# Layer 0 attention: the last query tile of all four heads of a quad turned by VectorE and sent through DRAM, and the token-shift difference of the second norm made in place

## Chip, cores, metric

One core of one Trainium2 chip. The metric is the device time of one execution in microseconds (us), the median of several runs.

## What is computed

Two adaptive-layernorm layers follow each other on x of 8 batches, 512 tokens, 256 features. Only the first one is touched. Cut to what matters:

```python
h = layernorm(x) * (1 + ca) + sa
q, k, v = heads(h @ q_w), heads(h @ k_w), heads(h @ v_w)      # 16 heads of 16
scores = q @ k.T / 4 - slope[h] * |i - j|                     # causal, 512 x 512 for each head
x = x + ga * (softmax(scores) @ v) @ o_w
h = layernorm(x) * (1 + cb) + sb
h_prev = shift h by one token, zeros first
xr = mu_r * h + (1 - mu_r) * h_prev                           # = h_prev + mu_r * (h - h_prev)
xk = mu_k * h + (1 - mu_k) * h_prev
x = x + gb * sigmoid(xr @ W_r.T) * (square(relu(xk @ W_k.T)) @ W_v.T)
```

The second layer (local and linear attention, an MLP, four times over; then grouped attention and a mixture of experts) makes up the rest of the time and keeps its code.

## The kernel before

Everything is float32. Each engine has its own instruction stream, written out by hand, and waits on semaphores. Layer 0 runs over slots: slot n = 4b + q works on batch b and on quad q, four heads at a time, 32 slots in all, and a few short slots behind them finish the last batches. A slot holds three kinds of work that are interleaved.

Of its own quad, per slot n. TensorE makes the scores in three units (`scores`, L746), whose PSUM banks S are shared: unit 0 is query tile 3 (four heads, 512 keys wide), unit 1 is tiles 2 and 0 (384 and 128 wide), unit 2 is tile 1 (256 wide). Each unit overwrites banks that the unit before it filled, so it waits for VectorE to have read them. VectorE reads them in `shifted` (L510): one custom instruction per head and tile adds the mask, writes the sum to `prob` and gives the row minimum. ScalarE exponentiates in place (`exps`, L649). At the end of the slot VectorE turns the first three heads of tile 3 in 32x32 blocks into `wide_blocks` (`turn_wide`, L520).

Of the quad before, m = n - 1. The softmax weights must lie key by query for the product with v. Head 3 of tile 3 and all heads of tiles 2, 0 and 1 are turned by TensorE (`turn_probs`, L762, one 128x128 transpose per key block) in eight groups, the list `TURNED`, into two PSUM banks H that alternate; each group is copied to SBUF by ScalarE (groups in `ON_ACT`) or VectorE (`evacuate`, L294), and the group after next waits for that copy. The three heads turned by VectorE go to DRAM and back on SP's queue (`move_wide`, L353 four writes, L358 one read), which puts the 32x32 blocks where they belong (`wideT`). TensorE then forms the product with v for all of them (`values`, L782, "AV"), the last large work of the slot.

Of other batches, six `parts` of one or two steps a slot (`work_of`): projections Q, K, V of the next batch, the turning and normalising of the attention's output (OT, BT, OUT), the second norm's transposes (L2), and the feed-forward products (KF, RF, VF). They use two banks M in turn, and a step waits for the step two before it to be read out. The steps read out by VectorE are OT (L534, L535), OUT (L544, L547) and VF (L565, L568).

So within a slot TensorE's stream is: scores unit 0, groups 0 and 1, part 0, groups 2 and 3, part 1, group 4, part 2, scores unit 1, groups 5 and 6, part 3, group 7, scores unit 2, part 4, part 5 with AV. VectorE's is: `shifted` of two heads of tile 3, group 1, the other two heads, part 0, norm, part 1, group 3, part 2, `shifted` of tiles 2 and 0, part 3, group 6, `shifted` of tile 1, part 4, `turn_wide`, statistics (L485, L488), norm (L496), `mixed` (L556), part 5.

Of the feed-forward part, GpSimd makes `diff` = h - h_prev (L434) in slots with q = 1, VectorE makes xk from it at the end of that slot and xr at the end of the next (`mixed`), and KF and RF read them from `mixT`.

Of the kernel before, what the change touches and what calls it, by code (L numbers as in the profile page):

```python
# [22 lines left out]
P = 128  # L23
B = 8
T = 512
NT = T // P
D = 256
KD = D // P
# [95 lines left out]
SLOTS = B * QUADS  # L124
ORDER_T = (3, 2, 0, 1)
FROM = (0, P, 3 * P, 6 * P)
ROUND = 3
SQUARE = 32
GROUPS = P // SQUARE
WIDE = ROUND * NT  # L130
TURNED = [(3, j, 1) for j in range(ROUND, 4)] + [(2, j, 1) for j in range(4)] + [(0, 0, 4)] + [(1, j, 2) for j in (0, 2)]
ON_ACT = (0, 2, 4, 5, 7)
PTS = len(TURNED)


# [57 lines left out]
def layer0(c, d, start):  # L193
    nc = c.nc
    s = c.s
    with ExitStack() as st:
        def sb(name, shape, dt=F32):
            return st.enter_context(nc.sbuf_tensor(name, shape, dt))
# [3 lines left out]
        mu = sb("mu0", [P, 2, KD])  # L202
        h2T = sb("h2T0", [P, KD, T + 1])
        mixT = sb("mixT0", [P, 2, KD, T])
        diff = sb("diff0", [P, KD, T])
        kact = sb("kact0", [P, KD, T])
        rsig = sb("rsig0", [P, NT, D])
        wqkv = sb("wqkv0", [P, 3, KD, D])
# [18 lines left out]
        tmp = spare[:, 7168:8192].rearrange("p (i t n) -> p i t n", i=2, n=D)  # L227
        wideT = probT[:, 0:P * WIDE].rearrange("p (i k r) -> p i k r", i=GROUPS, r=SQUARE)
        lowT = probT[:, P * WIDE:P * WIDE + 4 * 768].rearrange("p (j n) -> p j n", j=4)
        lastT = probT[:, P * WIDE + 4 * 768:4 * 1280].rearrange("p (j n) -> p j n", n=T)  # L230
        by_block = "p (k n) -> p k n"
        wm = [[spare[:, 7168:8192].rearrange(by_block, k=KD), spare[:, 5120:6144].rearrange(by_block, k=KD),
               spare[:, 6144:7168].rearrange(by_block, k=KD)], [mixT[:, 0], mixT[:, 1], kact[:, :, :]]]
        wide = "p i n -> p (i n)"
        rows = [[gates[0:B, 0].rearrange(wide), gates[0:B, 1].rearrange(wide), rsig[0:B, 2:4, :].rearrange(wide)],
                [diff[0:B, 0, :], diff[0:B, 1, :], rsig[0:B, 0:2, :].rearrange(wide)]]
        sign = tmp[0:B, 0, 0, :]
        qP = [c.prob[:, 4 * i:4 * i + 4, :] for i in range(2)]
        kP = [c.probT[:, 4 * i:4 * i + 4, :] for i in range(2)]
# [45 lines left out]
        def evacuate(eng, copy, m, k):  # L285

            tile, j, nj = TURNED[k]
            at = PTS * m + k
            eng.wait_ge(s["pt_full0"], at + 1)
            if m:  # L290
                full(eng, ("AV", m - 1, 0))
            width = P * (tile + 1)
            dst = lowT[:, j:j + nj, FROM[tile]:FROM[tile] + width] if tile < 3 else lastT[:, j - ROUND:j - ROUND + nj, :]
            copy(dst,  # L294
                 H[at % 2][:, 0:nj * width].rearrange("p (j n) -> p j n", j=nj))\
                .then_inc(s[("pt_out0", "pt_out1")[at % 2]], 1)

        @block.sync
        def _(sp):
# [47 lines left out]
            def move_wide(m):  # L347
                sp.wait_ge(s["wide_turned"], ROUND * (m + 1))
                if m:
                    sp.wait_ge(s["wide_in"], 16 * m)  # L350
                for i in range(GROUPS):
                    src = blocks[SQUARE * i:SQUARE * (i + 1), :, :, :].rearrange("p a k r -> p a (k r)")
                    sp.dma_start(c.probs_dram[0][:, :, i, :].rearrange("a p n -> p a n"), src)\  # L353
                      .then_inc(s["wide_away"], 16)
                sp.wait_ge(s["wide_away"], 16 * GROUPS * (m + 1))
                if m:
                    full(sp, ("AV", m - 1, 0))
                sp.dma_start(wideT.rearrange("p i k r -> p (i k r)"),  # L358
                             c.probs_dram[0].rearrange("a p i n -> (a p) (i n)")).then_inc(s["wide_in"], 16)

            for n in range(SLOTS + 2 * QUADS):
                b, q = divmod(n, QUADS)
# [26 lines left out]
        def _(pool):  # L389
# [35 lines left out]
            for n in range(ALL_SLOTS):  # L425
                b, q = divmod(n, QUADS)
                side = side_of(n)
                for f in side["norm"]:
                    rstd(f, "statsf", "rstdf")
                for f in side["diff"]:  # L430
                    drained(pool, ("L2", 0, f))
                    drained(pool, ("L2", 1, f))
                    pool.wait_ge(s["mixed_ready"], 2 * f)
                    nc.gpsimd.tensor_tensor(diff[:, :, :], h2T[:, :, 1:T + 1], h2T[:, :, 0:T], ALU.subtract)\  # L434
                      .then_inc(s["diff_ready"], 1)
                for f in side["square"]:
                    drained(pool, ("KF", 0, f))
                    drained(pool, ("KF", 1, f))
                    nc.gpsimd.tensor_tensor(kact[:, :, :], kact[:, :, :], kact[:, :, :], ALU.mult)\
                      .then_inc(s["squared_ready"], 1)  # L440
                for f in side["gate"]:
                    drained(pool, ("RF", 0, f))
                    drained(pool, ("RF", 1, f))
                    pool.wait_ge(s[("gb_loaded0", "gb_loaded1")[f % 2]], 16 * (f // 2 + 1))
                    steps(nc.gpsimd.tensor_scalar(rsig[:, :, :], rsig[:, :, :], 1.0, 0.5, ALU.add, ALU.mult))
                    row = gates[:, 1, f % 2:f % 2 + 1, :].to_broadcast([P, NT, D])
                    nc.gpsimd.tensor_tensor(rsig[:, :, :], rsig[:, :, :], row, ALU.mult).then_inc(s["gated0"], 1)
                if q == 0 and b + 2 < B:
                    rstd(b + 2)

        @block.vector
        def _(dve):
# [47 lines left out]
            def shifted(n, u, i, heads):  # L500

                tile, at = UNITS[u][i]
                width = P * (tile + 1)
                dve.wait_ge(s["scores_full"], 3 * n + u + 1)
                for j in heads:
                    if n and tile == 3 and j < ROUND:
                        dve.wait_ge(s["wide_turned"], ROUND * (n - 1) + j + 1)
                    elif n:
                        dve.wait_ge(s["pt_full0"], PTS * (n - 1) + 1 + turn_of(tile, j))
                    nc.vector.tensor_tensor_reduce(out=prob[:, j, FROM[tile]:FROM[tile] + width],  # L510
                                                   in0=S[:, j, at:at + width], in1=mask[:, T - width:T], scale=1.0,
                                                   scalar=3e38, op0=ALU.add, op1=ALU.min,
                                                   accum_out=least[:, n % 2, tile, j:j + 1]).then_inc(s["least0"], 1)
# [84 lines left out]
            for n in range(ALL_SLOTS):  # L598
# [18 lines left out]
                    shifted(n, 1, 0, range(4))  # L617
                    shifted(n, 1, 1, range(4))
                taken(parts[3])
                turned(m, (6,))  # L620
                if live:
                    shifted(n, 2, 0, range(4))
                taken(parts[4])
# [17 lines left out]
        def _(act):  # L641
# [61 lines left out]
            for n in range(ALL_SLOTS):  # L703
# [10 lines left out]
                    exps(n, 0, 0, (2, 3))  # L714
                turned(m, (4,))
                taken(parts[2])
                turned(m, (5,))
                if live:
                    exps(n, 1, 0, range(4))
                taken(parts[3])  # L720
                turned(m, (7,))
                if live:
                    exps(n, 1, 1, range(4))
                taken(parts[4])
# [5 lines left out]
        def _(pe):  # L730
# [35 lines left out]
            def values(m, bank):  # L766
# [3 lines left out]
                for tile in range(NT):  # L770
                    if tile == 3:
                        pe.wait_ge(s["wide_in"], 16 * (m + 1))
                    for key in range(tile + 1):
                        for j in range(4):
                            src = FROM[tile] + P * key
                            if tile < 3:
                                moving = lowT[:, j, src:src + P]
                            elif j < ROUND:
                                moving = wideT[:, :, NT * j + key, :]
                            else:  # L780
                                moving = lastT[:, j - ROUND, P * key:P * key + P]
                            ins = nc.tensor.matmul(bank[32 * j:32 * j + 32, tile * P:(tile + 1) * P],  # L782
                                                   vt[:, b % 2, key, 4 * q + j, :], moving,
                                                   start=(key == 0), stop=(key == tile), tile_position=(0, 32 * j))
# [92 lines left out]
            for n in range(ALL_SLOTS):  # L877
# [15 lines left out]
                if live:  # L893
                    scores(n, 1)
                if turns:
                    turn_probs(m, (5, 6))
                work(parts[3])
                if turns:
                    turn_probs(m, (7,))
                if live:  # L900
                    scores(n, 2)
                work(parts[4])
# [1893 lines left out]
```

## Time and profile before

| | |
|---|---|
| median of 3 runs | 2836.78 us (2836.17 to 2840.8) |
| the profiled execution | 2835.08 us, its span 2833.1 us |
| mean granted TensorE clock | 0.982 of full |
| busy, share of span | PE 96%, DVE 61%, ACT 49%, POOL 29% |
| the 32 slots | first scores at 29.9 us, slot 31 ends at 543.3 us |
| a full batch of four slots | 65.38 us (298.39 to 363.77 us) |

PE is TensorE's matmuls, PEld its weight loads, DVE VectorE, ACT ScalarE, POOL GpSimd. A row of the timeline gives start, duration, engine, line, operation, how many instructions are merged in it, and in brackets how long the engine was idle before it and what released it. A float32 matmul shows as two records, a transpose as one. Matmuls overlap their neighbours, so a merged row is about 0.1 us longer than the step from its start to the next start. A row of the windows has the stretch, its length, the busy time of PE, PEld, DVE, ACT and POOL with instruction counts, the granted clock (1.00 is 2.4 GHz, 0.50 is 1.2 GHz), the DMA share and GB/s.

### The profile page before, as it was taken

The numbers are of one execution on the slowest core, as the hardware profiler recorded it, in microseconds if no ns is written. First come the engines' busy times: TensorE is split into PE (matmuls) and PEld (weight loads), VectorE is DVE, ScalarE is ACT, GpSimd is POOL, SyncE is SP. The second block draws the span as 40 slices with busy tenths as digits, with TensorE's granted clock in tenths as the row PEclk, the third lists the DMA queues.
The fourth block names the chain that finished last, engine by engine and source line by source line (L and its number), as shares of the span: only waits on it lengthen the run. The fifth ranks groups of instructions, "written<-read, shape, count | busy, mean of one in ns | idle before, by whom it ended". The sixth has DMA issues, their size and how long they took to land. (4 is left out here: it accounts for less than half of the span.)

```text
span 2833.1 us, 50970 instructions
## 1 busy us (share of the span) xinstructions
PE 2706.5 (96%) x19124; PEld 1808.2 (64%) x19124; DVE 1727.5 (61%) x5112; ACT 1378.7 (49%) x3081; POOL 820.5 (29%) x830
## 2 busy tenths in 40 slices
PE   7999999887999999999999999999999887899998
PEld 4667776654566666666666666666666444578886
DVE  5888887778766555556565656566745788711113
ACT  4777777524554545555555454545541332322224
POOL 1001111124433332323232333333331210045551
PEclk9999999998999999999999999999999988999999
DMA  6544443325545455545455555454540000123325
GB/s 191 134 122 109 120 124 105 100 75 173 162 120 158 134 167 158 159 126 168 139 168 152 149 155 149 145 156 129 145 124 26 12 16 30 60 68 82 74 76 200
DMA packets 241380, 344.48 MB, mean 122 GB/s; under 512 B 25635, under 2 KB 174118, under 8 KB 237024
## 3 DMA queue, kind: packets, MB, share of 16 engines
q1 hardware_dynamic: 232304, 320.71, 39.0%
q0 software_dynamic: 7680, 16.32, 2.3%
q10 hardware_dynamic: 1152, 4.19, 0.4%
q8 instruction: 152, 2.49, 0.4%
q14 instruction: 92, 0.75, 0.1%
HBM read 184.61 MB, written 152.67 MB: 119 GB/s over the span
## 5 line engine op out<-in xcount | busy, mean ns | idle before, releaser
L1664 PE MATMUL bank<-w,gT 128*128 128x256 f32 x2048 | 463.5, 382 | 2.6 <-ACT gT L1582 2.6
L1631 PE MATMUL bank<-h2T,w 128*128 128x512 f32 x1024 | 444.7, 592 | 0.0
L1664 PEld LDWEIGHTS bank<-w,gT 128*128 128x128 f32 x2048 | 383.8, 190 | 75.9 <-issue 24.9
L1582 ACT ACTIVATE gT<-bank,vec 128x512 f32<-128x512 f32 x256 | 175.9, 687 | 389.6 <-PE bank L1631 389.6
L1631 PEld LDWEIGHTS bank<-h2T,w 128*128 128x128 f32 x1024 | 194.6, 190 | 231.3 <-issue 229.6
L1216 POOL TENSOR_TENSOR prob<-prob,rsum 128x512 f32<-128x512 f32 (+1 forms) x256 | 233.2, 933 | 212.7 <-DVE rsum L1428 211.6
L510 DVE CUSTOM_DVE_ANT_0 y<-bank,mask 128x128 f32<-128x128 f32 (+3 forms) x512 | 219.6, 484 | 64.5 <-PE bank L746 64.1
L649 ACT ACTIVATE y<-y,least 128x128 f32<-128x128 f32 (+3 forms) x512 | 248.4, 560 | 10.7 <-DVE least L510 10.6
L1405 DVE CUSTOM_DVE_ANT_0 prob<-bank,mask 128x256 f32<-128x256 f32 (+1 forms) x512 | 164.3, 387 | 124.3 <-PE bank L1619 124.3
L1523 ACT ACTIVATE prob<-prob,least 128x256 f32<-128x256 f32 (+1 forms) x512 | 238.7, 469 | 1.8 <-DVE least L1405 1.8
L1602 PE MATMUL bank<-wtok,hT 128*128 128x512 f32 x512 | 225.3, 592 | 2.1 <-ACT hT L1514 1.3
L2542 DVE COPY yout<-bank 128x512 f32<-128x512 f32 x40 | 27.7, 692 | 257.0 <-PE bank L2674 250.3
L1602 PEld LDWEIGHTS bank<-wtok,hT 128*128 128x128 f32 x512 | 97.1, 190 | 124.2 <-issue 122.5
L1246 POOL TENSOR_TENSOR tok<-tok,qinv 128x512 f32<-128x512 f32 x32 | 43.7, 1365 | 415.3 <-DVE qinv L1386 415.3
L1302 DVE STREAM_TRANSPOSE prob_blocks<-prob 128x1024 f32<-128x1024 f32 (+1 forms) x128 | 141.3, 1104 | 15.1 <-POOL prob L1216 15.0
L1281 DVE TENSOR_SCALAR xn<-y,mv,rstd 128x256 f32<-128x256 f32 x256 | 88.5, 408 | 98.7 <-POOL rstd L1197 98.7
L762 PEld LDWEIGHTS bank<-ident,y 128*128 128x128 f32 x896 | 102.7, 143 | 71.4 <-issue 57.2
L1287 DVE STREAM_TRANSPOSE score<-xn 128x1024 f32<-128x1024 f32 x63 | 78.5, 1245 | 113.2 <-DMA turned_rows<-score 109.0
L2662 PE MATMUL bank<-inT,we 128*128 128x256 f32 x640 | 144.8, 379 | 2.5 <-ACT inT L2593 1.3
L2601 ACT ACTIVATE score<-bank 128x512 f32<-128x512 f32 x80 | 47.8, 597 | 204.3 <-PE bank L2662 204.3
L762 PE MATMUL bank<-ident,y 128*128 128x128 f32 x896 | 132.9, 281 | 12.8 <-DVE probT L294 6.6
L2674 PE MATMUL bank<-we,score 128*128 128x256 f32 x640 | 144.6, 379 | 0.0
(337 smaller groups left out, 4862.9 us busy)
## 6 DMA issues: line engine op xcount, KB each, us to landing
probT<-turned_probs SPq DMA_DIRECT2D x64, 768.0 KB, 5.0
turned_probs<-prob_blocks SPq DMA_DIRECT2D x128, 256.0 KB, 5.5
probT<-turned_probs SPq DMA_DIRECT2D x32, 1024.0 KB, 5.9
turned_rows<-score SPq DMA_DIRECT2D x252, 128.0 KB, 2.9
score<-turned_rows SPq DMA_DIRECT2D x63, 512.0 KB, 3.9
turned_probs<-wide_blocks SPq DMA_DIRECT2D x128, 192.0 KB, 3.1
turned_probs<-prob_blocks SPq DMA_DIRECT2D x128, 192.0 KB, 3.1
w<-in_W SPq DMA_DIRECT2D x8, 1024.0 KB, 8.4
```

Of the source, the lines that this page charges most:

```text
L510: nc.vector.tensor_tensor_reduce(out=prob[:, j, FROM[tile]:FROM[tile] + width], in0=S[:, j, at:at + width], in1=mask[:, T - width:T], scal ...
L649: ins = nc.scalar.activation(one, one, ACT.Exp, bias=least[:, n % 2, tile, j:j + 1], scale=-1.0)
L762: ins = nc.tensor.transpose(H[at % 2][:, col:col + P], prob[:, j0 + j, src:src + P], c.ident[:, :])
L1216: nc.gpsimd.tensor_tensor(two, two, rsum[:, at:at + 2].unsqueeze(2).to_broadcast([P, 2, width]), ALU.mult).then_inc(s["probs"], 1)
L1405: nc.vector.tensor_tensor_reduce(out=prob[:, at, from_col(q):PAIR], in0=S[:, j, off:off + width], in1=mask[:, from_col(q):PAIR], scale=1.0 ...
L1523: nc.scalar.activation(one, one, ACT.Exp, bias=least[:, at:at + 1], scale=-1.0, accum_out=sums[:, at:at + 1]).then_inc(s["exped"], 1)
L1582: nc.scalar.activation(gT[:, m, :], M[m % 2][:, :], ACT.Gelu, bias=vec[:, h // B, 4 * KD + m:4 * KD + m + 1])\
L1602: ins = nc.tensor.matmul(S[:, t, :], hT[:, k, 1 + t * P:1 + (t + 1) * P], wtok[:, k, :], start=(k == 0), stop=(k == KD - 1))
L1631: ins = nc.tensor.matmul(M[m % 2][:, :], w1[:, k, m * P:(m + 1) * P], h2T[:, k, :], start=(k == 0), stop=(k == KD - 1))
L1664: ins = nc.tensor.matmul(M[i][:, (t % 2) * D:(t % 2 + 1) * D], gT[:, m, t * P:(t + 1) * P], w2[:, m, :], start=(m == 0), stop=(m == MF - 1))
L2662: ins = nc.tensor.matmul(UP[(2 * j + i) % 4][:, (m % 2) * CHUNK_T:(m % 2 + 1) * CHUNK_T], w1[e % 2][:, k, m * P:(m + 1) * P], inT[j % 2][: ...
L2674: ins = nc.tensor.matmul(DOWN[j % 2][:, t * D:(t + 1) * D], gT[j % 2][:, k, t * P:(t + 1) * P], w2[e % 2][:, k, :], start=(k == 0), stop=( ...
```

## The change

- `ROUND` goes from 3 to 4: VectorE turns head 3 of tile 3 too (`turn_wide`, 128 x 512), and its product with v reads `wideT` like the others. The first entry of `TURNED` goes: TensorE no longer makes those four 128x128 transposes, ScalarE no longer copies their 128 x 512 result.
- The seven groups left move up: the slot's stream on TensorE has groups 0 and 1 (now three transposes each), 2 and 3, 4 (now the four of tile 0), and between scores unit 1 and unit 2 only group 5 and group 6. ScalarE copies groups 0, 2, 4 and 6, VectorE 1, 3 and 5 (of the same sizes as before).
- The transfers through DRAM grow by a third: four writes of 256 KB instead of 192 KB, one read of 1024 KB instead of 768 KB, through the other, larger scratch tensor.
- `diff` gets no tile of its own but lies in `mixT[:, 0]`, which the previous batch's RF reads; GpSimd waits for that RF, and xr is made in place over the difference. The rows of the modulation that lay in `diff` lie in `spare_rows` and `tmp`.

```diff
-ROUND = 3
+ROUND = 4
-TURNED = [(3, j, 1) for j in range(ROUND, 4)] + [(2, j, 1) for j in range(4)] + [(0, 0, 4)] + [(1, j, 2) for j in (0, 2)]
-ON_ACT = (0, 2, 4, 5, 7)
+TURNED = [(2, j, 1) for j in range(4)] + [(0, 0, 4)] + [(1, j, 2) for j in (0, 2)]
+ON_ACT = (0, 2, 4, 6)
...
-        diff = sb("diff0", [P, KD, T])
+        spare_rows = sb("spare_rows", [P, T])
...
-                [diff[0:B, 0, :], diff[0:B, 1, :], rsig[0:B, 0:2, :].rearrange(wide)]]
+                [spare_rows[0:B, :], tmp[0:B, 1].rearrange(wide), rsig[0:B, 0:2, :].rearrange(wide)]]
+        diff = mixT[:, 0]
...
-            dst = lowT[...] if tile < 3 else lastT[:, j - ROUND:j - ROUND + nj, :]
+            dst = lowT[:, j:j + nj, FROM[tile]:FROM[tile] + width]
...
-                    sp.dma_start(c.probs_dram[0][:, :, i, :].rearrange("a p n -> p a n"), src)\
+                    sp.dma_start(c.probs_dram[1][:, :, i, :].rearrange("a p n -> p a n"), src)\
...
+                    if f:
+                        full(pool, ("RF", 1, f - 1))
                     nc.gpsimd.tensor_tensor(diff[:, :, :], h2T[:, :, 1:T + 1], h2T[:, :, 0:T], ALU.subtract)\
...
-                    if n and tile == 3 and j < ROUND:
+                    if n and tile == 3:
                         dve.wait_ge(s["wide_turned"], ROUND * (n - 1) + j + 1)
...
(VectorE)      turned(m, (6,)) -> turned(m, (5,))
(ScalarE)      turned(m, (5,)) is gone, turned(m, (7,)) -> turned(m, (6,))
(TensorE, between scores(n, 1) and scores(n, 2))
-                    turn_probs(m, (5, 6))
+                    turn_probs(m, (5,))
                 work(parts[3])
-                    turn_probs(m, (7,))
+                    turn_probs(m, (6,))
```

## Rows read from the trace of the kernel before

**Rows 1.** Busy time of the whole span, from the page.
```profile
PE 2706.5 (96%) x19124; PEld 1808.2 (64%) x19124; DVE 1727.5 (61%) x5112; ACT 1378.7 (49%) x3081; POOL 820.5 (29%) x830
```

**Rows 2.** Windows: busy time in the slots with q = 1, 2, 3, 0.
```profile
298.39:315.19 16.80, 16.54 (x177) 11.67 (x173) 15.60 (x57) 12.25 (x27) 3.86 (x4) 1.00 0.39 110
315.19:331.90 16.71, 16.71 (x177) 11.66 (x173) 14.21 (x48) 12.83 (x27) 1.89 (x1) 1.00 0.60 135
331.90:348.77 16.87, 16.64 (x181) 13.20 (x180) 13.68 (x44) 12.71 (x27) 0.00 (x0) 1.00 0.32 88
348.77:363.77 15.00, 14.90 (x165) 10.23 (x164) 13.13 (x51) 12.44 (x26) 3.97 (x4) 1.00 0.56 142
```

**Rows 3.** Groups by shape on DVE, 298.39 to 363.77 us.
```profile
L520 DVE STREAM_TRANSPOSE wide_blocks<-y 128x512 f32<-128x512 f32 x13 | 8.2, 680 | 0.0
```

**Rows 4.** Timeline, PE, slot q = 2, from scores unit 1.
```profile
322.04 1.15 PE L746 MATMUL bank<-probT,prob 17*128 17x384 f32 x16
...
323.12 1.22 PE L762 MATMUL bank<-ident,y 128*128 128x128 f32 x8
...
324.17 1.88 PE L820 MATMUL bank<-mixT,wf 128*128 128x512 f32 x4
...
325.89 0.60 PE L762 MATMUL bank<-ident,y 128*128 128x128 f32 x4
...
326.42 0.71 PE L746 MATMUL bank<-probT,prob 17*128 17x256 f32 x8
```

**Rows 5.** Timeline, PE, scores unit 2 of four other slots.
```profile
106.05 1.33 PE L746 MATMUL bank<-probT,prob 17*128 17x256 f32 x8 [0.26 <-DVE least L510]
...
309.69 1.33 PE L746 MATMUL bank<-probT,prob 17*128 17x256 f32 x8 [0.22 <-DVE least L510]
...
343.30 0.71 PE L746 MATMUL bank<-probT,prob 17*128 17x256 f32 x8
...
360.05 0.71 PE L746 MATMUL bank<-probT,prob 17*128 17x256 f32 x8
```

**Rows 6.** Timeline, DVE, first and last reads of scores unit 1.
```profile
310.18 0.08 DVE L510 DVE_READ_ACCUMULATOR2_ANT least<- 128x1 f32 x1
...
323.25 0.56 DVE L510 CUSTOM_DVE_ANT_0 y<-bank,mask 128x384 f32<-128x384 f32 x1 [1.96 <-PE bank L746]
...
326.02 0.08 DVE L510 DVE_READ_ACCUMULATOR2_ANT least<- 128x1 f32 x1
...
342.74 0.08 DVE L510 DVE_READ_ACCUMULATOR2_ANT least<- 128x1 f32 x1
...
359.76 0.08 DVE L510 DVE_READ_ACCUMULATOR2_ANT least<- 128x1 f32 x1
```

**Rows 7.** Timeline, slot q = 1, where TensorE starts VF.
```profile
303.58 0.42 DVE L535 TENSOR_TENSOR y<-bank,den 128x256 f32<-128x256 f32 x1
...
304.06 1.59 PEld L830 LDWEIGHTS bank<-wf,kact 128*128 128x128 f32 x8 [0.28 <-DVE y L535]
```

**Rows 8.** Timeline, slot q = 0, where TensorE starts L2.
```profile
353.70 1.38 DVE L496 TENSOR_SCALAR xn<-x,mv,rstd 128x256 f32<-128x256 f32 x4
...
355.23 0.63 PE L815 MATMUL bank<-ident,xn 128*128 128x128 f32 x4
```

**Rows 9.** Timeline, slot q = 3, DVE before OUT.
```profile
338.10 0.69 DVE L544 TENSOR_TENSOR y<-bank,gates 128x512 f32<-128x512 f32 x1 [2.00 <-PE bank L869]
```

**Rows 10.** Through DRAM: landing (page), read issue and AV (timeline).
```profile
probT<-turned_probs SPq DMA_DIRECT2D x64, 768.0 KB, 5.0
...
320.20 0.34 SPq L358 DMA_DIRECT2D probT<-turned_probs  x1
...
328.99 2.39 PE L782 MATMUL bank<-probT,vt 128*32 128x128 f32 x80
```

**Rows 11.** Slot 28: a window with its clock, and transposes.
```profile
485.00:490.00 5.00, 4.02 (x25) 2.92 (x26) 2.14 (x7) 1.44 (x3) 0.00 (x0) 0.50 0.47 161
...
489.02 1.97 PE L762 MATMUL bank<-ident,y 128*128 128x128 f32 x8
```

More of the change, by code:

```diff
@@ L229, in layer0 @@
         lowT = probT[:, P * WIDE:P * WIDE + 4 * 768].rearrange("p (j n) -> p j n", j=4)
-        lastT = probT[:, P * WIDE + 4 * 768:4 * 1280].rearrange("p (j n) -> p j n", n=T)
         by_block = "p (k n) -> p k n"
@@ L292, in evacuate @@
             width = P * (tile + 1)
-            dst = lowT[:, j:j + nj, FROM[tile]:FROM[tile] + width] if tile < 3 else lastT[:, j - ROUND:j - ROUND + nj, :]
+            dst = lowT[:, j:j + nj, FROM[tile]:FROM[tile] + width]
             copy(dst,
@@ L358, in move_wide @@
                 sp.dma_start(wideT.rearrange("p i k r -> p (i k r)"),
-                             c.probs_dram[0].rearrange("a p i n -> (a p) (i n)")).then_inc(s["wide_in"], 16)
+                             c.probs_dram[1].rearrange("a p i n -> (a p) (i n)")).then_inc(s["wide_in"], 16)
             for n in range(SLOTS + 2 * QUADS):
@@ L619, in _ @@
                 taken(parts[3])
-                turned(m, (6,))
+                turned(m, (5,))
                 if live:
@@ L716, in _ @@
                 taken(parts[2])
-                turned(m, (5,))
                 if live:
@@ L720, in _ @@
                 taken(parts[3])
-                turned(m, (7,))
+                turned(m, (6,))
                 if live:
@@ L777, in values @@
                                 moving = lowT[:, j, src:src + P]
-                            elif j < ROUND:
+                            else:
                                 moving = wideT[:, :, NT * j + key, :]
-                            else:
-                                moving = lastT[:, j - ROUND, P * key:P * key + P]
                             ins = nc.tensor.matmul(bank[32 * j:32 * j + 32, tile * P:(tile + 1) * P],
```

## The prediction, made before the result

> **What bounds the kernel now.** I read the page first: TensorE is busy for 96% of the span [rows 1], so a change that takes matmuls away looks like a gain of its matmul time. Then I cut the stretch of the change into slots with the windows. In a full batch of four slots TensorE is busy for 64.79 of 65.38 us [rows 2], VectorE for 56.6 (15.60 + 14.21 + 13.68 + 13.13, 87%), and in the slot with q = 1 VectorE reaches 15.60 of 16.80 us. The reader is to see that two engines are nearly full and that they wait for each other in turn. So the busy share alone can't say what four transposes are worth. The timeline can: for each place where TensorE loses or VectorE gains an instruction I asked which of them the next step waits for.
>
> **What is removed: four transposes a slot on TensorE, between scores unit 1 and scores unit 2.** Before, groups 5, 6 and 7 stand there (4 transposes each), after, groups 5 and 6. Ahead of unit 1 stood 16 transposes in groups 0 to 4 (4 + 3 + 3 + 3 + 3) and stand 16 after it (3 + 3 + 3 + 3 + 4). Hence the whole saving falls in one gap. Its price: eight transposes take 1.22 us and four take 0.60 as merged rows [rows 4]; the step from the start of the four to unit 2 is 326.42 - 325.89 = 0.53. I take 0.57, with 0.53 and 0.61 as the ends.
>
> But unit 2 also waits for VectorE, which must read all of unit 1 first: four reads of 384 and four of 128 columns. In the slot with q = 2 it starts when unit 1 is there (323.25) and ends with the last read at 326.02 + 0.08 = 326.10 [rows 6]. How soon can unit 2 end after that? In the slot with q = 1 it is stretched to 1.33 us by the wait and ends at 311.02, which is 0.76 after the last read at 310.26 [rows 5, 6]. With this floor:
>
> - q = 1: unit 2 already ends at the floor. Gain 0.
> - q = 2: ends now at 326.42 + 0.71 = 327.13, floor 326.86. Gain 0.27.
> - q = 3: ends at 344.01, floor 342.82 + 0.76 = 343.58. Gain 0.43.
> - q = 0: ends at 360.76, floor 359.84 + 0.76 = 360.60. Gain 0.16.
>
> Sum 0.86 us for a full batch instead of 4 x 0.57 = 2.28. The rest turns into a wait of TensorE for VectorE.
>
> **What is added: one 128 x 512 transpose a slot on VectorE**, at the slot's end. 13 of them cost 8.2 us, 0.63 each [rows 3]; the ends are 0.60 and 0.68 (the mean of one). Everything behind it on VectorE is late by that, up to its next idle time. What is queued behind it is statistics, norm, `mixed`, the gated sums of part 5, then the reads of the next slot's unit 0, group 1 and part 0. Slot by slot:
>
> - q = 3 to q = 0: VectorE has no idle time until the norm. The norm ends at 355.08 and TensorE starts L2 on it at 355.23, with group 4 in front of it until the same moment [rows 8]. 0.63 late there gives a loss of 0.57.
> - q = 0 to q = 1: again no idle time until OT is read out at 303.58 + 0.42 = 304.00; VF needs that bank and starts at 304.06, with nothing else in between [rows 7]. Loss 0.63.
> - q = 1 to q = 2 and q = 2 to q = 3: VectorE then idles for 1.96 us and 2.00 us until unit 1 and OUT are there [rows 6, 9], and that hides 0.63. If this cover were gone, each would cost 0.63. Loss 0.
>
> Sum of the losses 1.2 us, net +0.34 us for a full batch.
>
> The Trainium skill speaks against the move (VectorE: DVE Perf Modes, "Rules for kernel authors"): a 128x128 transpose belongs on TensorE, VectorE only turns 32x32 blocks. The rows agree that nothing is cheaper on VectorE (0.63 against 0.57), and by that rule alone the sum would be 0.06 us a slot, 2 us in all, to the worse; where the engines wait for each other is what decides.
>
> **ScalarE** loses a 128 x 512 copy. It is busy for 12.2 to 12.8 us of a slot [rows 2] and sits behind both other engines; I count 0. Bounds: 0 and a gain of about 0.3 us in some ten slots where a transpose waits for its copy. VectorE's own copies keep their sizes.
>
> **Transfers.** The read is issued at 320.20, lands some 5.0 us later, and AV starts at 328.99 [rows 10]: 3.8 us to spare, and the query tile that needs it comes last in AV. A third more data adds at most a third of 5.0, 1.7 us, and the issue moves by 0.63. Hidden, cost 0; SP's next work, placing the heads of the next batch, has a slot or more to spare. If they weren't hidden it would be 32 times the excess.
>
> **The difference in place.** GpSimd's new wait is for RF of the batch before, which stands in part 3 of the slot before, ahead of the L2 that GpSimd waits for anyway. `mixed` has the same operand sizes and already waits for that RF. Nothing queued behind GpSimd's wait moves. Cost 0. Bounds: none to speak of, one instruction a batch.
>
> **The sum over layer 0.** Full batches are slots 12 to 24: three at +0.34 and slot 12 at +0.41, +1.4 us. Front, slots 1 to 11: unit 2 is often stalled already, of which one row stands (1.33 us at 106.05) [rows 5], so the gains are few (about 0.7), while the two losses of a batch fall in slots 5, 8, 9 and 10 (2.4): +1.7. Back, slots 25 to 31 and the end: no more statistics for a next batch are taken, which gives VectorE room, so the only loss is in slot 28 (0.6), and the gains are 0.27, 0.43, 0.2 and 0.45; in slot 28 the clock is at 0.50 (1.2 GHz) and eight transposes take 1.97 us [rows 11], so four give 1.0; at the end group 6 no longer waits for a copy, 0.4. Together -2.1. Sum +1.0 us. The profiled execution took 2835.08 us against the runs' median 2836.78, 1.7 us less, 0.06%; the sum moves both alike. Forecast 2837.8, rounded 2838 us.
>
> A measurement of this kernel tells 0.2%, 5.7 us, from no change.
>
> **Rivals.**
> - *TensorE is the bound, as its 96% say.* Then 32 x 0.57 = 18 us come off: 2818.5. For it: 64.79 of 65.38 us busy. Against: the four floors above, which allow 0.86 of 2.28. A smaller form, the gains as read and the losses hidden, gives about 7 x -0.86 = -6, 2831. It is right if unit 2 can start sooner behind the last read than I take. Both together 0.15.
> - *VectorE becomes the bound* (the other side). If its 0.63 is hidden nowhere and the gap before unit 2 gives nothing back, 32 x 0.63 = 20 us: 2857. With half the slots hiding it, 2847. It decides (over 5.7 us) from about ten slots more at 0.63 than I count. For it: VectorE at 93% of slot q = 1. Against: the idle times of 2 us. 0.20.
> - *The clock falls more often.* In slot 28 TensorE idles for VectorE's statistics and norm, and the next 5 us are granted 0.50 [rows 11]; what it works there takes double, some 2.5 us. A longer wait can lengthen that or make such a fall elsewhere. Two more falls give +5 on top of +1, 2843. The Trainium skill (TensorE: Matmul & The Clock Gate, "What's actually happening") has the slow clock as the state that activity lifts, and the trace agrees in slot 28. 0.04.
> - *The transfer is late*, 1 us in each slot: 2869. Against: 3.8 us to spare. 0.01.
>
> **Numbers.** The forecast 0.60, faster 0.15, slower 0.25. The likeliest case alone runs from 2832 to 2842 (gains and losses of a batch each off by a third, and ScalarE's 3 us). The range must reach towards both sides: 2830 to 2849.
>
> **What would show it.** In the profile after: unit 2 at 1.2 to 1.4 us with a wait for VectorE's reads in nearly every slot (shows the gap gives little); a batch of four slots at 65.7 us, from 64.5 (gains without losses) to 67.0 (losses without cover); 128 transposes fewer on TensorE; four block transposes at 2.5 us a slot; the VF of slot q = 1 and the L2 of slot q = 0 later behind the slot's start by 0.6; AV with no wait for a DMA. I am wrong if TensorE's order hides a wait that I read as work, or if a batch comes out under 65.0 us.

## The result, and the profile after

| | before | after |
|---|---|---|
| median | 2836.78 us (13 runs, 2835.2 to 2840.9) | 2844.49 us (13 runs, 2840.69 to 2847.32) |
| profiled execution, span | 2835.08 us, 2833.1 us | 2842.70 us, 2841.0 us |
| mean granted TensorE clock in it | 0.982 | 0.979 |

The ratio is 1.0023 with an interval of 1.0015 to 1.0031: slower, by about the 0.2% that a measurement can tell, and the whole interval lies above 1. The forecast of 2838 us was 6.5 us too low; its range, 2830 to 2849, held the time, and "slower" had been given 0.25.

The page after, busy times of the whole span:

```profile
PE 2702.7 (95%) x18996; PEld 1802.1 (63%) x18996; DVE 1749.0 (62%) x5144; ACT 1364.7 (48%) x3049; POOL 820.7 (29%) x830
```

Against [rows 1] TensorE has 128 instructions and 3.8 us less, VectorE 32 instructions and 21.5 us more. Less than the 18 us that 128 transposes are worth went from TensorE's busy time, because other rows grew: unit 2 of a slot with q = 2 counts 0.99 instead of 0.71 us with a wait inside it, and work at a lower clock counts for longer (both below).

**The middle, where every batch is alike.** Windows of the same four slots as in [rows 2], q = 1, 2, 3, 0 (stretch, length, busy PE, PEld, DVE, ACT, POOL, clock, DMA share, GB/s):

```profile
304.70:321.40 16.70, 15.46 (x148) 10.65 (x148) 15.50 (x57) 11.01 (x25) 3.82 (x4) 1.00 0.51 144
321.40:338.20 16.80, 16.80 (x198) 11.81 (x191) 15.19 (x48) 12.78 (x28) 1.89 (x1) 1.00 0.67 159
338.20:355.15 16.95, 16.83 (x184) 13.22 (x183) 14.68 (x47) 12.80 (x26) 0.00 (x0) 1.00 0.46 126
355.15:370.30 15.15, 14.62 (x161) 9.94 (x161) 13.47 (x52) 11.90 (x25) 4.01 (x4) 1.00 0.72 173
sum 65.60, PE 63.70 PEld 45.62 DVE 58.84 ACT 48.48 POOL 9.72; mean PE 15.93 PEld 11.40 DVE 14.71 ACT 12.12 POOL 2.43
```

The four windows are cut at places of their own, and only their sum is to be compared: a batch takes 65.60 us where it took 65.38 (forecast 65.7). What answers to [rows 4 to 7], the timeline of TensorE:

```profile
311.05 1.99 PE L829 MATMUL bank<-wf,kact 128*128 128x256 f32 x8
...
316.67 1.33 PE L747 MATMUL bank<-probT,prob 17*128 17x256 f32 x8 [0.66 <-DVE least L512]
...
332.87 0.99 PE L747 MATMUL bank<-probT,prob 17*128 17x256 f32 x8
...
349.47 0.82 PE L747 MATMUL bank<-probT,prob 17*128 17x256 f32 x8
...
362.09 0.63 PE L814 MATMUL bank<-ident,xn 128*128 128x128 f32 x4
...
366.48 0.98 PE L747 MATMUL bank<-probT,prob 17*128 17x256 f32 x8
```

and of VectorE, its last reads of scores unit 1 in those slots, and its four block transposes:

```profile
317.17 0.08 DVE L512 DVE_READ_ACCUMULATOR2_ANT least<- 128x1 f32 x1
...
333.02 0.08 DVE L512 DVE_READ_ACCUMULATOR2_ANT least<- 128x1 f32 x1
...
335.28 2.49 DVE L522 STREAM_TRANSPOSE wide_blocks<-y 128x512 f32<-128x512 f32 x4
...
349.46 0.08 DVE L512 DVE_READ_ACCUMULATOR2_ANT least<- 128x1 f32 x1
...
366.63 0.08 DVE L512 DVE_READ_ACCUMULATOR2_ANT least<- 128x1 f32 x1
```

The last unit-2 matmul ends 0.75, 0.76, 0.75 and 0.75 us after the last read (318.00 - 317.25, 333.86 - 333.10, 350.29 - 349.54, 367.46 - 366.71): all four slots stand on the floor. VF comes 6.35 us into its slot instead of 5.67, L2 7.04 instead of 6.46. In the middle the machine did what the sum said.

**The front.** Counted from the first scores of a slot, slots 1 to 9 take 5.6 us more than before, of the 6.9 by which slot 31 begins late. Two slots carry 3.2 of it. TensorE's timeline, slots 6 and 7:

```profile
134.51 1.33 PE L747 MATMUL bank<-probT,prob 17*128 17x256 f32 x8 [1.31 <-DVE least L512]
135.77 2.99 PE L843 MATMUL bank<-wqkv,hT 128*128 128x256 f32 x8
138.69 3.02 PE L781 MATMUL bank<-probT,vt 128*32 128x128 f32 x80
...
152.57 1.42 PE L747 MATMUL bank<-probT,prob 17*128 17x256 f32 x8 [1.16 <-DVE least L512]
153.92 3.55 PE L868 MATMUL bank<-wo,y 128*128 128x256 f32 x8
157.40 2.39 PE L781 MATMUL bank<-probT,vt 128*32 128x128 f32 x80
```

and the same places before:

```profile
133.30 1.33 PE L746 MATMUL bank<-probT,prob 17*128 17x256 f32 x8 [0.35 <-DVE least L510]
134.56 1.99 PE L844 MATMUL bank<-wqkv,hT 128*128 128x256 f32 x8
136.48 2.39 PE L782 MATMUL bank<-probT,vt 128*32 128x128 f32 x80
```

The wait for VectorE in front of unit 2 grew from 0.35 to 1.31 us, and behind it eight matmuls of K take 2.99 instead of 1.99 us and AV 3.02 instead of 2.39. AV's own shape, count and inputs are as before and nothing releases it late; its clock is what differs. Windows of after, with what the clock was there:

```profile
130.00:135.00 5.00, 3.65 (x36) 2.93 (x37) 3.59 (x18) 4.24 (x9) 0.00 (x0) 1.00 0.65 147
135.00:140.00 5.00, 5.00 (x43) 3.56 (x45) 4.82 (x17) 2.83 (x8) 0.00 (x0) 0.66 1.01 276
...
150.00:155.00 5.00, 3.73 (x30) 2.73 (x24) 4.62 (x23) 4.12 (x12) 0.00 (x0) 0.87 0.04 11
155.00:160.00 5.00, 5.00 (x90) 4.03 (x89) 2.95 (x8) 1.43 (x5) 0.00 (x0) 0.79 0.00 0
515.00:520.00 5.00, 3.80 (x85) 3.59 (x88) 4.97 (x16) 2.57 (x8) 0.00 (x0) 0.66 0.13 40
```

0.66, 0.87 and 0.79 are mixes of the two levels, 1.2 and 2.4 GHz. Before, all windows from 100 to 480 us are at 1.00. After, three falls are new: in slots 6, 7 and 29. Each lengthens the rest of its slot, by 1.63, 1.55 and 1.27 us. In slot 29 the waits ahead of the fall are 0.65 us before unit 2 (0.22 before the change) and 1.20 us before AV (1.20 before the change too).

### The profile page after: what moved, and what is told of

Same layout as the page of the kernel before. It is cut to its first block and busy times, and to the rows that moved or that the text cites. A ratio compares the mean times of both kernels' runs of the same rounds, so it can differ in the third digit from the quotient of the medians.

```text
span 2841.0 us, 50658 instructions
## 1 busy us (share of the span) xinstructions
PE 2702.7 (95%) x18996; PEld 1802.1 (63%) x18996; DVE 1749.0 (62%) x5144; ACT 1364.7 (48%) x3049; POOL 820.7 (29%) x830
## 5 line engine op out<-in xcount | busy, mean ns | idle before, releaser
L512 DVE CUSTOM_DVE_ANT_0 y<-bank,mask 128x128 f32<-128x128 f32 (+3 forms) x512 | 219.5, 484 | 55.3 <-PE bank L747 54.5
L763 PEld LDWEIGHTS bank<-ident,y 128*128 128x128 f32 x768 | 88.1, 143 | 78.0 <-issue 66.1
L763 PE MATMUL bank<-ident,y 128*128 128x128 f32 x768 | 118.6, 281 | 19.1 <-DVE probT L294 15.5
```

The costliest lines, as they stand in the source:

```text
L763: ins = nc.tensor.transpose(H[at % 2][:, col:col + P], prob[:, j0 + j, src:src + P], c.ident[:, :])
```

## The experiments

Each kernel from e1 on was timed side by side with the kernel before, on one chip, in one of four sessions (e1 to e4, e5 to e8, e9 to e11, e12); the medians of before were 2839.32, 2837.96, 2839.08 and 2837.93 us in them. After was timed earlier, against a before of 2836.78 us for whose runs (but the profiled one) no clock is on record, so its clock part is compared with the before of the four sessions. Every run lists its span and its mean granted clock. I split the time by them: **clock part** = span x (1 - clock), **the rest** = time - clock part, each the mean over a kernel's runs. The standard error of such a mean is 0.5 to 1.6 us (e10: 2.5). The four "before" means agree within 0.7 us in the clock part and 0.8 us in the rest; e1, which does the same work, lies 0.9 to 1.6 and 0.5 to 1.3 us from them, so less than about 1.6 us is no difference.

The split is bookkeeping: exact where TensorE works all the time, too much where it idles at the low level anyway. How much too much can be read behind layer 0, from the end of the last AV on, where all kernels have the same code. There the profile of after has 41.5 us of clock part and that of before 37.5, 4.0 more, but the stretch takes only 1.5 us longer (2274.75 against 2273.23 us). So a rise of the clock part is not the same amount of lost time, and part of it lies outside layer 0: from before to after +3.4 us up to the last AV and +4.0 behind it.

| kernel (runs) | median us | ratio [95%] | clock part | the rest |
|---|---|---|---|---|
| before (17 to 34 in a session) | 2837.9 to 2839.3 | | 55.1 to 55.7 | 2783.1 to 2783.8 |
| after (13) | 2844.49 | 1.0023 [1.0015, 1.0031] | 61.9 | 2782.7 |
| e1 in-place difference alone (12) | 2837.53 | 0.9998 [0.9989, 1.0008] | 54.1 | 2784.4 |
| e2 TensorE's and ScalarE's part alone (11) | 2836.74 | 0.9989 [0.9981, 0.9998] | 64.4 | 2772.3 |
| e3 VectorE's part alone (7) | 2848.78 | 1.0027 [1.0016, 1.0038] | 54.5 | 2793.7 |
| e4 after, 8 idle transposes in 3 slots (11) | 2844.95 | 1.0019 [1.0010, 1.0028] | 58.9 | 2786.0 |
| e5 after, transfers of three heads (12) | 2845.77 | 1.0022 [1.0012, 1.0032] | 61.6 | 2783.4 |
| e6 after, 8 idle transposes in 5 slots (12) | 2844.74 | 1.0020 [1.0009, 1.0031] | 57.8 | 2787.3 |
| e7 after, head 0 turned earlier (11) | 2845.43 | 1.0027 [1.0017, 1.0037] | 65.7 | 2780.3 |
| e8 e7 with e6's idle work (12) | 2843.40 | 1.0024 [1.0014, 1.0034] | 62.5 | 2782.2 |
| e9 e7, 4 idle transposes in 13 slots (12) | 2843.28 | 1.0014 [1.0005, 1.0022] | 59.4 | 2783.9 |
| e10 after with the same idle work (9) | 2846.88 | 1.0025 [1.0014, 1.0035] | 60.4 | 2786.2 |
| e11 e7, 4 idle transposes in 31 slots (12) | 2845.07 | 1.0019 [1.0010, 1.0028] | 60.4 | 2785.2 |
| e12 e9, head 0 early only where it has room (12) | 2837.83 | 1.0003 [0.9993, 1.0014] | 56.5 | 2782.6 |

**e1: the difference in place, alone.** Before, with this part of the change.

```diff
-        diff = sb("diff0", [P, KD, T])
+        spare_rows = sb("spare_rows", [P, T])
+        diff = mixT[:, 0]
...
+                    if f:
+                        full(pool, ("RF", 1, f - 1))
                     nc.gpsimd.tensor_tensor(diff[:, :, :], ...)
```

> The kernel before with the second part of the change alone: the difference made in mixT and GpSimd's wait for the earlier RF. My theory: nothing is added ahead of a step that waits, ratio to the kernel before 1.000 (within 0.001). Rival (the new wait or the in-place operation holds GpSimd or VectorE up): a part of the 7.7 us, from +2 us on.

Measured 0.9998 (0.9989 to 1.0008), and a batch is again 65.38 us. The runs show no cost of this edit.

**e2: TensorE's part alone.** After, with VectorE and the transfers left at three heads. ScalarE's copy is gone with the transposes, and the difference is made in place.

```diff
-                    turn_wide(n, range(ROUND))
+                    turn_wide(n, range(TURNS3))
...
-                                moving = wideT[:, :, NT * j + key, :]
+                                moving = wideT[:, :, NT * min(j, 2) + key, :]
```

> TensorE's four transposes and ScalarE's copy taken away, nothing given to VectorE or the transfers: they handle three heads as before, and head 3 of the last tile is multiplied with head 2's weights, so part of the output is not the reference's. Theory of the floors: unit 2 waits for VectorE's reads, so only the 6.8 us of the gap between units 1 and 2 come off, to about 2829 to 2830 us (a new fall of the clock may eat up to 3 of them). Rival (TensorE is the bound and the floors are not real): 32 x 0.57 = 18 us off, 2819 us.

Measured 2836.74 us, 2.6 us below the before of its session, where 2829 to 2830 meant some 7 below the median known then. A batch takes 64.38 us, 1.00 less: the three gains of 0.28, 0.43 and 0.17 us between unit 1 and unit 2, and a further 0.17 at the end of slot q = 0. So the floors hold, and TensorE as the bound (about 2819) is out. The rest fell by 11.5 us (2783.8 to 2772.3), and the clock part rose by 8.7 (55.7 to 64.4). VectorE has nothing added here, and the difference in place does nothing (e1): it is the removal of TensorE's work, with its copy on ScalarE, that lowers the clock. The two figures are the bookkeeping's, too large by what TensorE idles at 1.2 GHz: in the profiles the clock part is 6.8 us more than before up to the last AV, and 5.6 more behind it, where the time grew by 2.1. The mean time fell by 2.8 us (2839.57 to 2836.75).

By slots, e2's profile takes 4.9 us less than before in slots 10 to 27 and 6.3 us more in slots 1 to 9. Slots 1 and 8, which have more of the low clock, carry 3.45 and 3.08 of that; slot 29 has a fall as well (+1.48). But slots 6 and 7, where after has its falls, keep the clock here. TensorE's timeline of e2:

```profile
134.90 1.33 PE L748 MATMUL bank<-probT,prob 17*128 17x256 f32 x8 [1.31 <-DVE least L513]
136.16 1.99 PE L844 MATMUL bank<-wqkv,hT 128*128 128x256 f32 x8
...
151.33 1.33 PE L748 MATMUL bank<-probT,prob 17*128 17x256 f32 x8 [1.16 <-DVE least L513]
152.59 1.99 PE L869 MATMUL bank<-wo,y 128*128 128x256 f32 x8
```

The waits of 1.31 and 1.16 us are those of after, to the hundredth, no fall follows, and the two slots are no longer than before (-0.11 and 0.00 us). So such a wait is free as long as the clock stays, and it doesn't decide by itself whether the clock falls.

**e3: VectorE's part alone.** Before, in-place difference, and a fourth block transpose whose result nobody reads; TensorE keeps its transposes.

```diff
                     turn_wide(n, range(ROUND))
+                    nc.vector.transpose(out=dead[...], in_=prob[:, 3, FROM[3]:FROM[3] + T]...)\
+                      .then_inc(s["wide_turned"], 1)
```

> The kernel before (with the difference in place) and a fourth block transpose on VectorE in each slot whose result nobody reads; TensorE keeps its four transposes, the transfers their size. Theory: VectorE's 0.63 us reach the end at slots with q = 0 and q = 1 only, 32 slots give +8 to +9 us, 2845 us, and TensorE, which has as much work as before, is granted no new 1.2 GHz stretch in slots 6 and 7. Rival 1 (VectorE's delay is hidden, the loss comes from the larger transfers): within 2 us of before. Rival 2 (VectorE is the bound everywhere): +20 us.

Measured +9.5 us against the median of before in its session (by the ratio +7.7), a batch of 66.50 us (+1.12). The extra transposes cost what the losses said, and the mean clock part stays where it was (54.5). Slots 6 and 7 have no fall. Slot 29 has one in the profile, though TensorE has all its transposes and the same waits as before, 0.22 and 1.20 us; AV takes 4.02 us there instead of 2.39:

```profile
518.86 4.02 PE L792 MATMUL bank<-probT,vt 128*32 128x128 f32 x80 [1.20 <-DVE probT L296]
```

So the fall that after's profile has in slot 29 can't be laid to the removed work. The bookkeeping of the two halves together: the rest -11.5 + 9.9 = -1.6 us (after: -0.4 to -1.1), the clock part +8.7 - 1.2 = +7.5 (after: +6.2 to +6.8).

**e4, e6: work in the wait.** After, with eight transposes of no use ahead of group 5 in slots 6, 7 and 30 (e4, of probabilities), or in slots 4, 6, 7 and 8 and ahead of AV in slot 29 (e6, of the identity).

```diff
+                    if n in (4, 6, 7, 8):
+                        idle_turns(m)
                     turn_probs(m, (5,))
...
+                        if i + 1 in (29,):
+                            for _ in range(8):
+                                nc.tensor.transpose(bank[:, 0:P], c.ident[:, :], c.ident[:, :])
                         ins = values(i, bank)
```

> The changed kernel with eight idle transposes on TensorE in front of group 5 in slots 6, 7 and 30, where the changed kernel waits 0.65 to 1.3 us for VectorE's reads and then is granted a lower clock. Theory: the waits let the clock fall; filled, slots 6 and 7 are short again by 1.6 us each and slot 29 or 30 by 1.3, so 3 to 4.5 us come off: 2840 to 2841.5 us. Rival (the long stretches after unit 2 in these slots have another cause, such as the larger transfers, or the clock falls all the same): as the changed kernel, 2844.5 us.

> The changed kernel with eight idle transposes of the identity on TensorE ahead of group 5 in slots 4, 6, 7 and 8, and eight more ahead of AV in slot 29, the waits behind which a clock of 1.2 GHz was seen (slots 6, 7, 8 and 29 in one run or another). Theory: the clock stays up in slots 4 to 10 in this run, slots 6, 7 and 8 have their old length behind unit 2 (4.76, 4.76 and 2.8 us), and about 3 us come off the changed kernel: 2841.5 us. Rival (filling one wait only moves the fall to another slot): no less than 2843.5 us, with low clock between 100 and 240 us.

Both medians missed: 2844.95 and 2844.74 us. The clock answered in the filled slots, the total did not. Windows of e6 where after had 0.66, 0.79 and 0.66:

```profile
135.00:140.00 5.00, 4.63 (x86) 3.54 (x85) 4.81 (x15) 3.65 (x10) 0.00 (x0) 1.00 0.97 245
...
155.00:160.00 5.00, 5.00 (x92) 3.50 (x85) 4.93 (x13) 1.89 (x4) 0.00 (x0) 1.00 0.14 31
515.00:520.00 5.00, 5.00 (x96) 3.92 (x85) 5.00 (x13) 2.72 (x6) 0.00 (x0) 1.00 0.15 33
```

No window between 100 and 480 us is below 1.00. Against after the clock part fell by 4.1 us, and the rest rose by 4.6. The idle work itself is not what took the gain back, for the waits hid it. TensorE's timeline of e6, slot 6, unit 2 and the end of AV:

```profile
134.34 1.33 PE L747 MATMUL bank<-probT,prob 17*128 17x256 f32 x8 [0.44 <-DVE least L512]
...
139.41 1.08 PE L787 MATMUL bank<-probT,vt 128*32 128x128 f32 x32 [0.37 <-DMA probT<-turned_probs]
```

In slots 6, 7 and 8 the wait shrinks from 1.31, 1.16 and 1.21 us to 0.44, 0.34 and 0.43, and unit 2 starts as long behind unit 1 as in after (3.48 us in slot 6). Slots 1 to 9 take 3.2 us more than before instead of 5.6. What stands against this in e6's profile: AV now waits for the transfer through DRAM, 0.48, 0.53 and 0.37 us in slots 2, 4 and 6; and three stretches without idle work are longer than in after, slot 1 by 2.0 us, slot 28 by 1.0, and all that lies behind layer 0 by 3.0. Why the median did not move stays open. In e4 slots 6 and 7 keep the clock as well, but slot 8, whose wait of 1.21 us was not filled and had no fall in after, has one (its rest +1.61 us); clock part and rest moved by -3.0 and +3.3 us against after.

**e5: smaller transfers.** After, but three of the four heads are moved.

```diff
-                    src = blocks[SQUARE * i:SQUARE * (i + 1), :, :, :]...
+                    src = blocks[SQUARE * i:SQUARE * (i + 1), :, 0:3 * NT, :]...
-                                moving = wideT[:, :, NT * j + key, :]
+                                moving = wideT[:, :, NT * min(j, 2) + key, :]
```

> The changed kernel with four block transposes on VectorE but transfers of three heads (192 and 768 KB); head 3 of the last tile is multiplied with head 2's weights, so part of the output is not the reference's. Theory: the transfers are hidden, within 1.5 us of the changed kernel, slots 12 to 24 the same. Rival (the larger transfers hold AV up in slots 6 to 8, or slow the engines down): 2 to 4 us less than the changed kernel.

Measured 2845.77 us, a batch of 65.60; its profile has the falls of slots 6, 7 and 29 too, and more of the low clock in slots 1 and 8. So the larger transfers are not what after loses by. But they have far less to spare than in slot 18, where the forecast read its 3.8 us: in slot 6 of after the read is issued at 133.02 us and takes 6.4 us to land, while AV starts at 138.69 us, and that at the low clock. Five profiles with all four heads moved show AV waiting for the transfer, 0.23 to 0.64 us at a time, in slots 2, 4, 6 or 16 (e4, e6, e10, e11, e12).

**e7, e8: head 0's block transpose at another place.** It is issued in VectorE's idle time in the middle of the slot, before part 1 (q = 3), part 2 (q = 1) or the reads of unit 1 (q = 0 and 2), so that the end of a slot is as short as before.

```diff
+                if live and q == 3:
+                    turn_wide(n, (0,))
                 taken(parts[1])
...
+                if live and q == 1:
+                    turn_wide(n, (0,))
                 taken(parts[2])
+                if live and q in (0, 2):
+                    turn_wide(n, (0,))
...
-                    turn_wide(n, range(ROUND))
+                    turn_wide(n, range(1, ROUND))
```

> The changed kernel with VectorE's block transpose of head 0 moved from the slot's end into the slot's middle, where VectorE is idle for 1.0 to 2.0 us (before part 1, part 2 or unit 1, by q); three stay at the end, as in the kernel before. Theory: the 0.63 us no longer reach L2 and VF; a full batch falls from 65.60 to 64.4 to 64.6 us (before: 65.38), and the kernel to about 2836 us, with falls of the clock as the rest: 0.1% under or level with the kernel before. Rival (VectorE's place doesn't matter, the transfers or the sum of its work do): a full batch at 65.6 us, 2844 us.

> The moved transpose and the idle transposes together. Theory: the two losses add up and both go: 2832 to 2834 us, 0.1 to 0.2% under the kernel before. Rival (clock falls turn up elsewhere): as the moved transpose alone.

A batch takes 64.39 us, as with no transpose added at all (e2), so the place hides the 0.63 us whole. The median still misses, at 2845.43: the clock part is the highest of all, 65.7 us. In its profile slots 10 to 27 take 4.9 us less than before, and slots 1 to 9 take 12.1 us more. With the idle work of e8 the clock part is 3.2 us less and the rest 1.9 more (2843.40).

**e9, e10, e11: less idle work in more slots.** Four transposes of the identity instead of eight, in slots 1 to 9 and 28 to 31 (e9 on e7, e10 on after), or in all slots from 1 on (e11 on e7).

```diff
+                    if n in (1, 2, 3, 4, 5, 6, 7, 8, 9, 28, 29, 30, 31):
+                        idle_turns(m)
                     turn_probs(m, (5,))
```

> The moved block transpose of e7 and, in slots 1 to 9 and 28 to 31, four idle transposes of the identity between unit 1 and group 5, so that TensorE has as much to do there as in the kernel before. Theory: slots 10 to 27 take about 1.0 us a batch less than before (as in e7), and with TensorE's old load the clock does not fall between 100 and 240 us: 4 to 5 us under the kernel before, 2832 to 2834 us, ratio 0.998 to 0.999. Rival (the falls in e7 have another cause than TensorE's thinner load, such as VectorE's order): low clock between 100 and 180 us again, 2840 us or more.

> The changed kernel with the same idle transposes. Theory: only the losses behind VectorE are left, 9 us in the starts of unit 1 less the gains of slots 10 to 27, and no fall of the clock between 100 and 240 us: 2840 to 2842 us, 2 to 4 us less than the changed kernel. Rival (clock falls cost it nothing): 2844.5 us.

> The same as e9 with the four idle transposes in all slots from 1 on. It gives TensorE back everything that the change took away, and VectorE's transpose is where it is hidden. Theory: a full batch of four slots at 65.4 us, level with the kernel before (65.38), so that the 1 us a batch between e9 and this one is all that TensorE's four transposes are worth; ratio 1.000. Rival (the gain of e9's middle slots comes from ScalarE's missing copy or the order of the groups): a full batch at 64.8 us or less.

The medians are 2843.28, 2846.88 and 2845.07 us. e9 has some 6 us less of the clock part than e7 and 3.6 more of the rest; e10 differs from after by less in the clock part (1.5) than its own error. e10's profiled execution took 2840.53 us, within its expectation, its median did not: one profile is one draw.

e11 puts back, in every slot, the number of transposes that before had. Over slots 10 to 27 it takes 0.7 us less than before, where e9 takes 4.5 less. So nearly all of that gain is TensorE's four transposes, as the theory said. The four slots of [rows 2], 17 to 20, would mislead here: they take 64.81 us, as the rival said, but other batches take 65.02 (slots 12 to 15) and 65.17 (slots 20 to 23), and slot 16 is 1.06 us longer than before. TensorE waits there for the transfer, in the middle of AV:

```profile
304.64 1.08 PE L798 MATMUL bank<-probT,vt 128*32 128x128 f32 x32 [0.55 <-DMA probT<-turned_probs]
```

What is left is 0.2 to 0.4 us a batch, of which 0.17 stands behind unit 2 in slots with q = 0, in e2, e9 and e11 alike. All three lack the copy of the result on ScalarE, and it is what is left to have given it (argued, not tried).

e9 showed a price of the earlier place that e7's expectation lacked. VectorE's timeline, slots 5 and 31:

```profile
119.08 0.71 DVE L525 STREAM_TRANSPOSE wide_blocks<-y 128x512 f32<-128x512 f32 x1 [0.55 <-DMA turned_probs<-wide_blocks]
...
536.03 0.71 DVE L525 STREAM_TRANSPOSE wide_blocks<-y 128x512 f32<-128x512 f32 x1 [2.56 <-DMA turned_probs<-wide_blocks]
```

The block buffer is still being written out for the slot before. In slot 31 unit 2 comes 4.61 us later for it, behind a fall of the clock too. TensorE's timeline:

```profile
535.01 1.15 PE L758 MATMUL bank<-probT,prob 17*128 17x384 f32 x16
538.57 1.11 PE L782 MATMUL bank<-ident 128*128 128x128 f32 x4 [2.40 <-DVE probT L294]
539.47 1.06 PE L774 MATMUL bank<-ident,y 128*128 128x128 f32 x4
540.33 3.62 PE L846 MATMUL bank<-wf,mixT 128*128 128x256 f32 x8
```

**e12: fitted.** e9, with head 0 early at q = 0 and 2 everywhere, and at q = 1 and 3 in slots 10 to 28 only.

```diff
+                early = q in (0, 2) or 10 <= n <= 28
-                if live and q == 3:
+                if live and early and q == 3:
```

> e9 with the block transpose of head 0 kept at the slot's end in the odd slots outside 10 to 28, because there e9 showed VectorE waiting 0.6 to 2.6 us for the previous slot's writes to leave the block buffer before it may turn head 0. Theory: the middle slots keep their gain of about 1.0 us a batch (4.5 us from slot 10 to 28), the front costs 1 to 2 us, and slots 3, 5 and 31 lose the 1.1 to 4.6 us between units 1 and 2 that e9 has: 2835 to 2838 us, ratio 0.998 to 1.000. Rival (the front's loss comes from chance falls of the clock whatever the order is): 2842 us.

Measured 2837.83 us, ratio 1.0003 (0.9993 to 1.0014): level with before, so the loss is taken back and nothing is won. A batch is at 64.38 us, slots 10 to 27 gain 3.8 us, and slots 1 to 9 cost 6.7: unit 2 of slot 6 waits 2.30 us for VectorE's reads. No version beats before clearly (e2, at 0.9989, leaves part of the computation out).

## Why the prediction came out as it did

The likeliest case was "a batch gains 0.86 and loses 1.2 us, and the sum is +1.0". Its mechanism was right in the middle slots, one term of the sum was too small, and a rival with a chance of 0.04 happened beside it. That the range held the time was luck: it reached up to 2849 for VectorE as the bound, which did not happen.

- *Gains in the gap before unit 2.* Forecast 0, 0.27, 0.43 and 0.16 us, measured 0, 0.28, 0.44 and 0.17. The floor of 0.76 us held in all four slots.
- *Losses.* L2 in slot q = 0 forecast 0.57, measured 0.58; VF in slot q = 1 forecast 0.63, measured 0.68 (0.60 and 0.67 at unit 1). The two idle times of 2 us hid the rest; measured 0.03 and 0.
- *ScalarE at 0.* In slot q = 0 the step after unit 2 is 0.17 us shorter, which I had not counted; e2 has it too, so it comes with the removed part. Hence 65.60 us for a batch instead of 65.7. Over slots 10 to 27 the change is +0.07 us.
- *In-place difference, transfers at 0.* Right for after (e1, e5): no AV waits for a DMA in its profile. But "3.8 us to spare" held in slot 18 only; in slot 6 the read is issued at 133.02 instead of 129.82 us, and where the clock stays up there AV waits for it (0.37 us in e6).
- *Slots 12 to 24, +1.4.* Measured +0.9.
- *Back -2.1.* Slots 25 to 31 came to +0.4. Unit 2 did come 0.54 us earlier in slot 27 and 0.55 in slot 31, but the fall in slot 29 took 1.27, L2's lateness 0.59 in slot 28, and unit 1 of slot 31 was 0.82 later. (The fall in slot 29 also comes in e3, with nothing removed.)
- *Front, slots 1 to 11, +1.7: the step that failed.* Measured +5.7. I had looked there for gains and losses of a slot only. The gap in front of unit 2 had long been a wait with work in it; when the work went, the wait for VectorE grew to 1.31 and 1.16 us, and the clock fell right behind it. The falls in slots 6 and 7 make 3.2 of the 5.7 us. The other 2.5 are longer waits without a fall: in slot 5 group 3 waits 1.15 us for VectorE's copy and unit 1 comes 1.03 later, and slot 8 is 1.16 us longer.
- *The clock rival, 0.04, priced 2843.* Three falls instead of the two that it supposed, in the profile, 1.3 to 1.6 us each instead of 2.5, and a median of 2844.49. Over all runs the clock part is 6.2 to 6.8 us more than before and the rest 0.4 to 1.1 us less, where the sum had +1.0. Read as time this would make nearly the whole loss TensorE's clock, but it counts too much. By the slots of the one profile the three falls carry 4.5 of the 7.2 us by which slot 31 ends late; the other 2.7 are waits less gains, where the sum had +1.0.

The step named in advance, "a longer wait can make such a fall elsewhere", was argued from one row of slot 28 [rows 11]. Slots 1 to 9, which already had waits [rows 5], were where it had to be weighed, with more than 0.04.

**Shown:** the gains and losses by slot; that the removed part alone raises the mean clock part (e2, by 8.7 us) and the added part alone doesn't (e3). **Shown in single profiles only:** that work put into the wait is hidden there and keeps the clock up at that place (e4, e6). Of the medians only e9's is lower for it, ratio 1.0014 against 1.0027 of e7, with intervals that overlap. **Not settled:** which waits let the clock fall, and how much of the loss in the median is the clock's. Waits of 1.31 and 1.16 us in slots 6 and 7 end in falls in after and not in e2; the wait of 1.21 us in slot 8 ends in one in e2 and e4 and not in after; slot 29 falls in e3 at the waits of before. Runs of one kernel spread by up to 12.5 us (e7, e12). The profile of after is one execution, and the three falls seen in it stand for a cost that the runs show only as a mean. At the end of slot 31 after is 7.2 us behind, at the end of the last AV 6.4 and at the end of the program 7.9; the 1.5 us between, in code that is the same, come with 4.0 us more of the clock part.

## What to carry to other kernels

Before taking work off an engine that is 96% busy, find for each place the wait that ends last behind it. What is left of a gain may be the distance to the last read plus a fixed step, here 0.75 us. Then ask what the removed work covered: if it stood in a wait, the wait becomes longer, and TensorE may come out of it at 1.2 GHz, which here cost 1.6 us where the wait alone cost nothing. Whether it does, one profile can't tell: the same wait went either way. A transfer that had time to spare in one slot is to be looked at in the tightest one. Work moved to a second engine belongs into that engine's idle time, and its output buffer must be free by then.

## What the runs showed that I had not expected

- In e2 TensorE was relieved of 128 transposes, some 18 us by their rows, in a kernel whose other engines did nothing more. By the floors 6.8 us of it were to come off, the mean time fell by 2.8, and the clock part rose by 8.7.
- Such falls cost 1.3 to 1.6 us each in slots of 15 to 16 us, behind waits of 0.65 to 1.31 us for VectorE. The same waits stood in other kernels without a fall. Idle transposes kept the clock at 1.00 in their slots, and it fell in others.
- All kernels with head 0 turned early agree in the middle to 0.01 us a batch unless they have idle work there (64.39, 64.39, 64.38), and their medians differ by 7.6 us (e7, e12), mostly through slots 1 to 9.
